# A mixture of experts in which every token goes through its two chosen experts only, by scattered and gathered rows, in place of all eight experts with gates

## The chip, the cores and the metric

The program runs on one core of one Trainium2 chip. The core has TensorE (PE: matmuls and transposes), VectorE (DVE), ScalarE (ACT), GpSimd (POOL), and SyncE (SP), whose queue issues most transfers; 16 DMA engines move the data. Each engine works through its own list of instructions in order and waits on semaphores. A time is the device time in microseconds (us) of one execution; a kernel's time is the median of its runs.

## The reference

x has 8 batches of 1,024 tokens of 128 numbers. Two blocks with residuals follow each other; shift, scale and gate of each come from a small conditioning row per batch (`mod`).

```
h = layernorm(x) * (1 + ca) + sa
x = x + ga * attention(h)                       # linear attention, 8 heads, RoPE, 5-tap convolution of v, output gate
h = layernorm(x) * (1 + cb) + sb
logits = h @ Wg + bg                            # 8 experts
probs = softmax(logits / 5.0)
vals, idx = top_k(probs, 2)
gates = mask / (sum(mask) + 1e-9)               # mask: vals at the two chosen experts, 0 elsewhere
y = sum over e of gates[e] * (gelu(h @ W1[e] + b1[e]) @ W2[e] + b2[e])
x = x + gb * y
```

W1 is 8 x 128 x 256 and W2 8 x 256 x 128. Six of a token's eight gates are zero. All inputs and the output are float32.

## The kernel before

All weights lie in SBUF, W1, W2 and the projections as a high and a low part (`w_h`, `w_l`) in the format float32r. `split` (L471 to L473) makes one product of full accuracy from three matmuls: high by high, low by high, high by low. A batch is 8 tiles (`J`) of 128 tokens, in two halves (`CH`) of 512 tokens (`CT`).

*Attention* runs in stages: statistics and normalisation of x (VectorE L834, L840, L846; the reciprocal root by `pow` on POOL, L755 and L758), transposes (L466), modulation on ScalarE into a high part and a copy (L639, L641), the low part on POOL (L771), the q, k, v projection per tile, the products with cosine and sine on VectorE (L878, L879) and their sum on POOL (L776), the k-v product (L502), denominators (L514) and numerators (L519), `heads` normalised by L910, five convolution steps (L1005, L1009), the gate, the output projection (L543) and x1 (L923). A second normalisation, transposes and logits (L558) follow, then the routing: softmax through tanh, a comparison of all pairs of experts, and the gates (L947 to L993).

*The experts* are 16 units a batch (`UNITS`): one half of the tokens by one expert. A unit is: layer 1 on PE (6 matmuls of 512 columns into `ps_h`), gelu on ScalarE (L702), multiplication by the gates on VectorE (L1019, `hid_g`; the gates come broadcast over all partitions from DRAM into `spread`), a high copy on ScalarE (L709, `hid_h`), the low part by subtraction on POOL (L807, `hid_l`), and layer 2 on PE (6 matmuls, L592 to L594), which adds up over the eight experts in `ps_y`. The result is turned back (L466) and added to x1 (L1030).

*The order* is written out by hand. A tick is one unit. `TICK` names the attention stages of the next batch that a tick issues, `LATE` the routing stages of the current one; layer 1 of a unit comes 8 ticks after its own tick (`SHIFT`), layer 2 three later (`LAG`). `schedule` (L141) walks all engines through the same ticks; the middle batches run in a hardware loop. Three PSUM banks (`ring`) go round among the attention stages.

## Time and profile before

| | us |
|---|---|
| three runs | 705.43, 706.93, 3041.11 |
| median | 706.93 |
| span of the profiled execution | 704.5 |

The span goes from the first to the last instruction; the page gives no time beside it for this execution, and the two close runs stand 0.9 and 2.4 us above it. The third run lies far off and no row explains it. A row of a group names line, engine, operation, what is written and read, the shape and the count; in a timeline the first number is the start in us and the second how long the row's instructions took together. VectorE is DVE in the rows, the queue of SyncE is SPq. A float32 matmul that isn't float32r leaves two records.

### The profile page before, as it was taken

How to read it: one execution, taken by the hardware profiler on the slowest of the kernel's cores; microseconds unless marked ns; L12 is line 12 of the kernel's file. 1: busy time of each engine (PE TensorE's matmuls, PEld its weight loads, DVE VectorE, ACT ScalarE, POOL GpSimd, SP SyncE). 2: the span in 40 equal slices, each digit the busy share in tenths (PEclk: the TensorE clock that was granted, in tenths of full speed). 3: DMA queues.
4: the chain of work that ended last, by engine and by line, in shares of the span. 5: the costliest groups of instructions: out<-in, count | busy, mean ns of one | idle time of the engine just before them, and what ended most of it. 6: DMA issues, size and time to landing. Idle time of an engine off the chain costs nothing.

```text
span 704.5 us, 9302 instructions
## 1 busy us (share of the span) xinstructions
PE 590.6 (84%) x2750; PEld 473.8 (67%) x2750; DVE 534.0 (76%) x1029; ACT 402.9 (57%) x639; POOL 450.5 (64%) x311
## 2 busy tenths in 40 slices
PE   4823897799987988789987989879887989889996
PEld 3623775587776866678765867668665777667884
DVE  5686677977889678787789778796798877884442
ACT  2331565566565746656565746657556655765773
POOL 3372555685866936857667838569458666665885
PEclk9975798899999989989999989999999989998999
DMA  6000341035100441008010341004210180004300
GB/s 239 2 30 0 127 125 31 1 98 168 45 1 15 128 124 45 1 17 247 15 30 14 113 138 45 1 15 158 91 45 0 34 230 15 1 15 169 96 16 15
DMA packets 37682, 47.57 MB, mean 68 GB/s; under 512 B 2096, under 2 KB 20432, under 8 KB 37392
## 3 DMA queue, kind: packets, MB, share of 16 engines
q1 hardware_dynamic: 37216, 46.77, 21.8%
q10 hardware_dynamic: 432, 0.43, 0.2%
q14 instruction: 23, 0.19, 0.1%
q8 instruction: 11, 0.18, 0.1%
HBM read 42.21 MB, written 4.98 MB: 67 GB/s over the span
## 4 chain that ended last, share of the span: by engine, by line
PE 30%; POOL 24%; DVE 21%; issue 17%; ACT 5%; POOLq 1%; DMA 1%; DVEq 0%; SPq 0%; ACTq 0%
POOL hid_l L807 20%; PE ring L466 4%; PE ring L519 3%; DVE xn L846 3%; DVE conv L1005 3%; DVE stats L834 3%; PE ps_y L592 3%; PE ring L514 3%; PE ps_y L593 3%; PE ps_y L594 2%; PE ps_h L471 2%; PE ps_h L472 2%; PE ps_h L473 2%; PE ring L558 2%; DVE hid_g L1019 2%
## 5 line engine op out<-in xcount | busy, mean ns | idle before, releaser
L807 POOL TENSOR_TENSOR hid_l<-hid_g,hid_h 128x1024 fp32r<-128x1024 f32 x128 | 304.9, 2389 | 147.4 <-ACT hid_h L709 138.4
L702 ACT ACTIVATE ps_h<-ps_h,b_f 128x512 f32<-128x512 f32 x256 | 158.5, 658 | 109.0 <-PE ps_h L473 108.3
L1019 DVE TENSOR_TENSOR hid_g<-ps_h,spread 128x1024 f32<-128x1024 f32 x128 | 155.5, 1216 | 71.1 <-POOL hid_l L807 58.2
L709 ACT ACTIVATE hid_h<-hid_g 128x1024 fp32r<-128x1024 f32 x128 | 135.5, 1058 | 11.7 <-DVE hid_g L1019 11.7
L592 PE MATMUL ps_y<-hid_h,w_h 128*128 128x512 f32 x256 | 114.3, 446 | 2.4 <-POOL hid_l L807 2.4
L471 PE MATMUL ps_h<-h_h,w_h 128*128 128x512 f32 x256 | 105.4, 412 | 9.2 <-DVE hid_g L1019 9.2
L593 PE MATMUL ps_y<-hid_h,w_l 128*128 128x512 f32 x256 | 106.0, 414 | 0.0
L594 PE MATMUL ps_y<-hid_l,w_h 128*128 128x512 f32 x256 | 105.8, 413 | 0.0
L472 PE MATMUL ps_h<-h_h,w_l 128*128 128x512 f32 x256 | 102.4, 400 | 0.0
L473 PE MATMUL ps_h<-h_l,w_h 128*128 128x512 f32 x256 | 102.1, 399 | 0.0
L466 PE MATMUL ring<-consts_f,xn 128*128 128x128 f32 x128 | 27.7, 362 | 63.4 <-DVE xn L846 62.2
L466 PEld LDWEIGHTS ring<-consts_f,xn 128*128 128x128 f32 x128 | 19.1, 182 | 73.2 <-DVE xn L846 58.1
L471 PEld LDWEIGHTS ps_h<-h_h,w_h 128*128 128x128 f32 x256 | 49.7, 194 | 24.5 <-DVE hid_g L1019 13.6
L592 PEld LDWEIGHTS ps_y<-hid_h,w_h 128*128 128x128 f32 x256 | 52.9, 207 | 16.0 <-POOL hid_l L807 3.7
L593 PEld LDWEIGHTS ps_y<-hid_h,w_l 128*128 128x128 f32 x256 | 52.0, 203 | 12.8 <-issue 3.0
L594 PEld LDWEIGHTS ps_y<-hid_l,w_h 128*128 128x128 f32 x256 | 51.4, 201 | 12.5
L472 PEld LDWEIGHTS ps_h<-h_h,w_l 128*128 128x128 f32 x256 | 49.4, 193 | 11.1 <-issue 0.2
L473 PEld LDWEIGHTS ps_h<-h_l,w_h 128*128 128x128 f32 x256 | 48.8, 191 | 11.8
L846 DVE TENSOR_SCALAR xn<-x,mean_var,rstd 128x128 f32<-128x128 f32 x64 | 54.7, 924 | 0.1
L776 POOL TENSOR_TENSOR qk<-qk_cos,qk_sin 128x256 f32<-128x256 f32 x64 | 46.7, 746 | 8.5 <-DVE qk_sin L879 8.4
L771 POOL TENSOR_TENSOR h_l<-heads,h_h 128x512 fp32r<-128x512 f32 x16 | 20.6, 1289 | 43.4 <-ACT heads L641 43.2
L1009 DVE SCALAR_TENSOR_TENSOR conv<-v_t,lepe_f,conv 128x1024 f32<-128x1024 f32 x32 | 44.2, 1382 | 0.3
(127 smaller groups left out, 929.9 us busy)
## 6 DMA issues: line engine op xcount, KB each, us to landing
spread<-gates_dram SPq DMA_DIRECT2D x16, 2048.0 KB, 8.9
xs<-in_x SPq DMA_DIRECT2D x8, 512.0 KB, 3.9
out<-y SPq DMA_DIRECT2D x16, 256.0 KB, 2.3
spread<-in_w SPq DMA_DIRECT2D x2, 1024.0 KB, 6.8
gates_e<-parts_dram SPq DMA_DIRECT2D x24, 32.0 KB
ga<-ga_dram SPq DMA_DIRECT2D x1, 512.0 KB, 3.6
spread<-in_wmod SPq DMA_DIRECT2D x1, 384.0 KB, 5.1
spread<-in_wqkvg ACTq DMA_DIRECT2D x1, 256.0 KB, 5.3
```

Of the source, the lines that this page charges most:

```text
L466: last = pe.transpose(dst[:, j * P:(j + 1) * P], src(j), ident)
L471: pe.matmul(dst, wh, ah, start=True, stop=False)
L472: pe.matmul(dst, wl, ah, start=False, stop=False)
L473: return pe.matmul(dst, wh, al, start=False, stop=True)
L592: pe.matmul(ps_y[:, :], w2_h[:, e, g, :], high, start=False, stop=False)
L593: pe.matmul(ps_y[:, :], w2_l[:, e, g, :], high, start=False, stop=False)
L594: last = pe.matmul(ps_y[:, :], w2_h[:, e, g, :], low, start=False, stop=(e == E - 1 and g == HH - 1))
L702: last = act.activation(bank, bank, ACT.Gelu, bias=b1_f[:, e, g:g + 1])
L709: act.activation(hid_h[n % 4][:, :, :], hid_g[n % 2][:, :, :], ACT.Copy)\
L807: pool.tensor_tensor(hid_l[n % 4][:, :, :], hid_g[n % 2][:, :, :], hid_h[n % 4][:, :, :].bitcast(F32), ALU.subtract).then_inc(s_hl, 1)
L846: last = dve.tensor_scalar(xn[:, j, :], src[:, j, :], mean_var[:, j, 0:1], rstd[:, j:j + 1], ALU.subtract, ALU.mult)
L1019: dve.tensor_tensor(hid_g[n % 2][:, :, :], ps_h[n % HIDDEN][:, :, :], gates_all[c][:, e, :].unsqueeze(1).to_broadcast([P, HH, CT]), ALU.mu ...
```

## The change

Nothing of the reference is left out. Attention keeps its computation, with some operations put together and more buffers. The routing finds the two chosen experts as two one-hot masks (`hot`), in `choose`. A prefix sum by matmuls (`prefix`) and `put` give each pair of token and choice a row number in a list ordered by expert, in which every expert's rows start at a multiple of 128. The list has 23 tiles of 128 rows for any choice (`TILES`). For each of 8 token tiles and 2 choices POOL scatters 128 rows of the normalised x1 to `x_sort` in DRAM (`scat`, 16 transfers a batch). SP loads the rows back in groups of four tiles (`xg`), and for each tile reads the expert's number from SBUF into a register and loads its W1, W2 and b1 (128 x 514 numbers) into one of 8 buffers (`w`). PE transposes the rows (`xsT`), ScalarE modulates them; layer 1, gelu and layer 2 run on tiles in pairs (`l1`, `l2`), with plain float32 matmuls of 128 columns and no gates. ScalarE evicts (`oev`), SP stores to `o_sort` (`ost`), POOL gathers two rows for each token (`gat`, 16 transfers), and VectorE multiplies them with the two gates and adds (`comb`, `fin`). The bias b2 comes by one matmul for each half. `AT` gives every stage its tick; batches start 24 ticks apart (`T`), the program has no loop, and within a tick the older batch comes first.

```diff
-TICK = {0: [], 1: ["norm1_0", "norm1_1"], 2: ["norm1_apply0", "norm1_apply1", "modulate"],
-        3: ["xT0"], 4: ["xT1", "qkv0"], 5: ["qkv1"], 6: ["qkv2"], 7: ["qkv3"], 8: ["vT"],
-        9: ["kv", "qT", "den_num"], 10: ["rdenT"], 11: ["gate"], 12: ["out0", "out1"],
-        13: ["norm2_apply0", "norm2_apply1"], 14: ["x1T0", "x1T1"], 15: ["logit"]}
...
-LATE = {0: ["softmax0"], 2: ["softmax1"], 3: ["rank0"], 4: ["rank1", "choice"], 5: ["gatesT"]}
...
+TILES = (TOP * S + E * (P - 1)) // P
+ROWS = TILES * P
+GROUP = 4
+GROUPS = -(-TILES // GROUP)
+PAIRS = -(-TILES // 2)
...
+T = 24
+FFN = 41
+AT = {"load": -24, "stat1_0": -6, "stat1_1": -5, "pow1": -5, "app1_0": -3, "app1_1": -3, "xT_0": -2, "xT_1": -1,
+      "qkv_0": 0, "qkv_1": 1, "qkv_2": 2, "qkv_3": 3, "vT": 4, "kv": 5, "qT": 5, "den": 6, "dn_0": 7, "dn_1": 7,
+      "conv_0": 8, "conv_1": 9, "conv_2": 10, "conv_3": 11, "gate": 11, "conv_4": 12,
+      "out_0": 13, "out_1": 14, "stat2_0": 15, "stat2_1": 16, "pow2": 16, "app2_0": 17, "app2_1": 18,
+      "x1T_0": 18, "x1T_1": 19, "logit": 20, "choose": 21, "prefix": 22, "soft": 23, "place": 24, "gT": 25}
+AT |= {f"scat_{j}": 28 + j for j in range(J)}
+AT |= {f"w_{t}": FFN + t - 3 for t in range(TILES)}
+AT |= {f"xg_{g}": (FFN - 3 + g if g < 3 else FFN - 1 + GROUP * (g - 3)) for g in range(GROUPS)}
+AT |= {f"xsT_{g}": FFN - 2 + GROUP * g for g in range(GROUPS)}
+AT |= {f"l1_{h}": FFN + 2 * h for h in range(PAIRS)}
+AT |= {f"l2_{h}": FFN + 2 * h + 3 for h in range(PAIRS)}
+AT |= {f"oev_{g}": FFN + GROUP * g + 6 for g in range(GROUPS)}
+AT |= {f"ost_{g}": FFN + GROUP * g + 7 for g in range(GROUPS)}
+AT |= {f"gat_{j}": 70 + j for j in range(J)}
+AT |= {"b2_0": 76, "b2_1": 81, "fin_0": 81, "fin_1": 85, "store_0": 82, "store_1": 86}
+AT |= {f"comb_{j}": 77 + j for j in range(J)}
+FIRST, LAST = min(AT.values()), max(AT.values())
+TABLE = {n: [name for name, at in AT.items() if at == n] for n in range(FIRST, LAST + 1)}
...
+def schedule(stage):
+    for tick in range(FIRST, T * (B - 1) + LAST + 1):
+        for b in range(B):
+            for name in TABLE.get(tick - T * b, []):
+                kind, _, n = name.partition("_")
+                stage(b, kind, int(n) if n else 0)
...
+                elif kind == "w":
+                    k = nth(b, n)
+                    if n == 0:
+                        sp.wait_ge(s_owner, b + 1)
+                    if k >= W_RING:
+                        old_b, old_t = divmod(k - W_RING, TILES)
+                        sp.wait_ge(s_l2, couple(old_b, old_t // 2) + 1)
+                    e = sp.value_load(owner[b % 2][0:1, n:n + 1], min_val=0, max_val=E - 1)
+                    sp.dma_start(wbuf[k % W_RING][:, :], w_all[bass.ds(e, 1)].rearrange("a p f -> (a p) f"))\
+                        .then_inc(s_wb[k % W_RING], 16)
+                elif kind == "xg":
+                    k, first = group(b, n), n * GROUP
+                    many = min(GROUP, TILES - first)
+                    if n == 0:
+                        sp.wait_ge(s_scat[b % 2], 16 * TOP * J * (b // 2 + 1))
+                    if k >= XG_RING:
+                        sp.wait_ge(s_xsT, k - XG_RING + 1)
+                    sp.dma_start(xg[k % XG_RING][:, 0:many, :],
+                                 x_sort[b % 2][first * P:(first + many) * P, :].rearrange("(t p) d -> p t d", p=P))\
+                        .then_inc(s_xg[k % XG_RING], 16)
+                elif kind == "ost":
+                    k, first = group(b, n), n * GROUP
+                    many = min(GROUP, TILES - first)
+                    sp.wait_ge(s_oe, k + 1)
+                    sp.dma_start(o_sort[b % 2][first * P:(first + many) * P, :].rearrange("(t p) d -> p t d", p=P),
+                                 o_s[k % O_RING][:, 0:many, :]).then_inc(s_os[k % O_RING], 16)
...
-            def layer1(f, n):
-                c, e = divmod(n, E)
-                if n == 0:
-                    pe.wait_ge(s_h2l, f.count(CH, CH))
-                if not (f.first and n < HIDDEN):
-                    pe.wait_ge(s_hg, f.count(UNITS, n + 1 - HIDDEN))
-                t = slice(c * CT, (c + 1) * CT)
-                for g in range(HH):
-                    w = slice(g * P, (g + 1) * P)
-                    last = split(ps_h[n % HIDDEN][:, g, :], w1_h[:, e, w], w1_l[:, e, w],
-                                 h2_h[f.par][:, t], h2_l[f.par][:, t])
-                last.then_inc(s_l1, 1)
...
-                pe.wait_ge(s_hl, f.count(UNITS, n + 1))
-                for g in range(HH):
-                    high, low = hid_h[n % 4][:, g, :], hid_l[n % 4][:, g, :]
-                    pe.matmul(ps_y[:, :], w2_h[:, e, g, :], high, start=False, stop=False)
-                    pe.matmul(ps_y[:, :], w2_l[:, e, g, :], high, start=False, stop=False)
-                    last = pe.matmul(ps_y[:, :], w2_h[:, e, g, :], low, start=False,
-                                     stop=(e == E - 1 and g == HH - 1))
-                last.then_inc(s_l2, 1)
...
+                elif kind == "xsT":
+                    k = group(b, n)
+                    pe.wait_ge(s_xg[k % XG_RING], ring_count(k, XG_RING))
+                    if k >= 1:
+                        pe.wait_ge(s_xs, k)
+                    for t in range(min(GROUP, TILES - n * GROUP)):
+                        last = pe.transpose(ps_x[:, t * P:(t + 1) * P], xg[k % XG_RING][:, t, :], ident)
+                    last.then_inc(s_xsT, 1)
+                elif kind == "l1":
+                    k, g = couple(b, n), group(b, 2 * n // GROUP)
+                    pe.wait_ge(s_xs, g + 1)
+                    if k >= 2:
+                        pe.wait_ge(s_gelu, k - 1)
+                    for m in couple_tiles(n):
+                        w = nth(b, m)
+                        pe.wait_ge(s_wb[w % W_RING], ring_count(w, W_RING))
+                        t = slice(m % GROUP * P, (m % GROUP + 1) * P)
+                        for h in range(HH):
+                            last = pe.matmul(ps_hid[k % 2][:, m % 2, h, :], wbuf[w % W_RING][:, h * P:(h + 1) * P],
+                                             xs_t[g % XS_RING][:, t], start=True, stop=True)
+                    last.then_inc(s_l1, 1)
+                elif kind == "l2":
+                    k, g = couple(b, n), group(b, 2 * n // GROUP)
+                    pe.wait_ge(s_gelu, k + 1)
+                    if g >= 1:
+                        pe.wait_ge(s_oe, g)
+                    for m in couple_tiles(n):
+                        w = nth(b, m)
+                        for h in range(HH):
+                            last = pe.matmul(ps_o[:, m % GROUP, :], hid[k % HID_RING][:, m % 2, h, :],
+                                             wbuf[w % W_RING][:, HID + h * D:HID + (h + 1) * D], start=(h == 0),
+                                             stop=(h == HH - 1))
+                    last.then_inc(s_l2, 1)
...
-            def high_part(f, n):
-                act.wait_ge(s_hg, f.count(UNITS, n + 1))
-                if not (f.first and n < 4):
-                    act.wait_ge(s_l2, f.count(UNITS, n - 3))
-                act.activation(hid_h[n % 4][:, :, :], hid_g[n % 2][:, :, :], ACT.Copy)\
-                    .then_inc(s_hh, 1)
...
+                elif kind == "l1":
+                    k = couple(b, n)
+                    act.wait_ge(s_l1, k + 1)
+                    if k >= HID_RING:
+                        act.wait_ge(s_l2, k - HID_RING + 1)
+                    for m in couple_tiles(n):
+                        w = wbuf[nth(b, m) % W_RING]
+                        for h in range(HH):
+                            last = act.activation(hid[k % HID_RING][:, m % 2, h, :], ps_hid[k % 2][:, m % 2, h, :],
+                                                  ACT.Gelu, bias=w[:, 2 * HID + h:2 * HID + h + 1])
+                    last.then_inc(s_gelu, 1)
...
-            def low_part(f, n):
-                pool.wait_ge(s_hh, f.count(UNITS, n + 1))
-                if not (f.first and n < 4):
-                    pool.wait_ge(s_l2, f.count(UNITS, n - 3))
-                pool.tensor_tensor(hid_l[n % 4][:, :, :], hid_g[n % 2][:, :, :],
-                                   hid_h[n % 4][:, :, :].bitcast(F32), ALU.subtract).then_inc(s_hl, 1)
...
+                elif kind == "scat":
+                    if n == 0:
+                        pool.wait_ge(s_slot, b + 1)
+                        if b == 0:
+                            pool.wait_ge(s_zero, 16 * 2 * GROUPS)
+                        if b >= 2:
+                            pool.wait_ge(s_xsT, group(b - 1, 0))
+                    for k in range(TOP):
+                        at = slots[b % 4][:, k * J + n:k * J + n + 1]
+                        pool.indirect_dma_start(x_sort[i], bass.IndirectOffsetOnAxis(ap=at, axis=0), xn2[i][:, n, :],
+                                                None).then_inc(s_scat[i], 16)
+                elif kind == "gat":
+                    if n == 0:
+                        for r in range(O_RING):
+                            pool.wait_ge(s_os[r], 16 * len(range(r, group(b + 1, 0), O_RING)))
+                        if b >= 1:
+                            pool.wait_ge(s_comb, J * b)
+                    for k in range(TOP):
+                        at = slots[b % 4][:, k * J + n:k * J + n + 1]
+                        pool.indirect_dma_start(og[:, k, n, :], None, o_sort[i],
+                                                bass.IndirectOffsetOnAxis(ap=at, axis=0)).then_inc(s_gat[n], 16)
...
-            def gate_hidden(f, n):
-                c, e = divmod(n, E)
-                if e == 0:
-                    dve.wait_ge(s_gall[c], f.count(16, 16))
-                dve.wait_ge(s_gelu, f.count(UNITS, n + 1))
-                if not (f.first and n < 2):
-                    dve.wait_ge(s_hl, f.count(UNITS, n - 1))
-                dve.tensor_tensor(hid_g[n % 2][:, :, :], ps_h[n % HIDDEN][:, :, :],
-                                  gates_all[c][:, e, :].unsqueeze(1).to_broadcast([P, HH, CT]),
-                                  ALU.mult).then_inc(s_hg, 1)
...
+            def choose(b):
+                dve.wait_ge(s_lg, b + 1)
+                step(b, 1, dve.tensor_tensor(logit[:, :, :], lg_ps.rearrange("p (j e) -> p j e", e=E), by_tile(br_f[:, :]),
+                                             ALU.add))
...
+                step(b, 13, dve.tensor_tensor(chosen[:, 0:J * E], hot[:, 0, :], hot[:, 1, :], ALU.add))
...
+            def put(b):
...
+                step(b, 34, dve.tensor_reduce(slots[b % 4][:, :], picked[:, :, :].rearrange("p k (j e) -> p (k j) e", e=E),
+                                              AX_X, ALU.add))
+                dve.sem_inc(s_slot, 1)
...
+                step(b, 37, dve.tensor_reduce(owner[b % 2][:, :], past[:, :, :], AX_X, ALU.add))
+                dve.sem_inc(s_owner, 1)
...
+                elif kind == "comb":
+                    c = n // JC
+                    dve.wait_ge(s_gat[n], 16 * TOP * (b + 1))
+                    if n % JC == 0:
+                        dve.wait_ge(s_b2, CH * b + c + 1)
+                    g = gate2[b % 4]
+                    dve.scalar_tensor_tensor(u[:, n, :], og[:, 0, n, :], g[:, 0, n:n + 1],
+                                             ps_z[:, n % JC * D:(n % JC + 1) * D], ALU.mult, ALU.add).then_inc(s_fin, 1)
+                    dve.wait_ge(s_fin, (J + CH) * b + c * (JC + 1) + n % JC + 1)
+                    dve.scalar_tensor_tensor(u[:, n, :], og[:, 1, n, :], g[:, 1, n:n + 1], u[:, n, :], ALU.mult, ALU.add)\
+                        .then_inc(s_comb, 1)
...```

The order on POOL, where the low part and the q-k sums of the next attention stand. Before, from one batch's experts:

```order
L807 TENSOR_TENSOR hid_l<-hid_g,hid_h 128x1024
L769 ISA
L771 TENSOR_TENSOR h_l<-heads,h_h 128x512
L804 REGISTER_ALU
L806 REGISTER_ALU
L807 TENSOR_TENSOR hid_l<-hid_g,hid_h 128x1024
L769 REGISTER_ALU
L771 TENSOR_TENSOR h_l<-heads,h_h 128x512
```

And in the changed kernel, one batch's steps from the powers to the last scatters (`og` is filled by gathers, `x_sort` by scatters; x2 is one token tile, x14 seven):

```order
L607 TENSOR_TENSOR rstd<-var_eps,minus_half 128x8
L652 DMA og<-o_sort,slots 128x128 x2
L622 TENSOR_TENSOR h_l<-h_f,h_h 128x512
L652 DMA og<-o_sort,slots 128x128 x2
L622 TENSOR_TENSOR h_l<-h_f,h_h 128x512
L652 DMA og<-o_sort,slots 128x128 x2
L626 TENSOR_TENSOR qk<-qk_cos,qk_sin 128x512
L652 DMA og<-o_sort,slots 128x128 x2
L626 TENSOR_TENSOR qk<-qk_cos,qk_sin 128x512
L652 DMA og<-o_sort,slots 128x128 x2
L626 TENSOR_TENSOR qk<-qk_cos,qk_sin 128x512
L652 DMA og<-o_sort,slots 128x128 x2
```

```order
L626 TENSOR_TENSOR qk<-qk_cos,qk_sin 128x512
L652 DMA og<-o_sort,slots 128x128 x2
L642 DMA x_sort<-xn_0,slots 2944x128 x2
L652 DMA og<-o_sort,slots 128x128 x2
L642 DMA x_sort<-xn_0,slots 2944x128 x14
L605 TENSOR_TENSOR var_eps<-mv,eps_ln 128x8
L607 TENSOR_TENSOR rstd<-var_eps,minus_half 128x8
```

The second piece follows the first without a gap. The subtractions of the experts are gone from POOL; between the low parts and the sums that attention needs stand gathers of a batch three further back, and ahead of the next power the scatters of the batch in between.

The order on PE beside the logits. Before:

```order
L471 MATMUL ps_h<-h_h,w_h 128x512
L472 MATMUL ps_h<-h_h,w_l 128x512
L473 MATMUL ps_h<-h_l,w_h 128x512
L558 MATMUL ring<-wr_f,heads 128x8 x8
L592 MATMUL ps_y<-hid_h,w_h 128x512
L593 MATMUL ps_y<-hid_h,w_l 128x512
L594 MATMUL ps_y<-hid_l,w_h 128x512
```

Changed:

```order
L409 MATMUL bank<-consts_f,xn_1 128x128 x4
L461 MATMUL ps_o<-wbuf,hid 128x128 x4
L417 MATMUL ps_z<-wr_f,h_t 128x8 x8
L450 MATMUL ps_hid<-xs_t,wbuf 128x128 x4
L461 MATMUL ps_o<-wbuf,hid 128x128 x4
```

Each unit of twelve matmuls of 512 columns has become a pair of tiles with four and four of 128.

## Rows read from the trace of the kernel before

**Rows 1.** The profile's page, part 1: busy us (share of the span), instructions.
```profile
PE 590.6 (84%) x2750; PEld 473.8 (67%) x2750; DVE 534.0 (76%) x1029; ACT 402.9 (57%) x639; POOL 450.5 (64%) x311
```

**Rows 2.** Stretches: length, busy us (PE, PEld, DVE, ACT, POOL), clock, DMA share, GB/s.
```profile
38.00:100.00 62.00, 36.23 (x176) 29.22 (x177) 47.35 (x114) 23.12 (x43) 29.49 (x27) 0.72 0.26 80
220.60:300.20 79.60, 69.57 (x332) 55.65 (x331) 62.77 (x117) 48.07 (x78) 54.65 (x38) 0.95 0.24 69
618.60:704.50 85.90, 74.40 (x303) 58.17 (x303) 40.34 (x40) 53.63 (x74) 58.20 (x26) 0.93 0.20 64
```

**Rows 3.** The timeline of SP's queue: start us, us, what is issued; loads of x.
```profile
106.16 0.41 SPq L395 DMA_DIRECT2D xs<-in_x  x1
...
515.15 0.38 SPq L395 DMA_DIRECT2D xs<-in_x  x1
```

**Rows 4.** Groups of instructions by line: busy us, mean ns of one; idle before.
```profile
L807 POOL TENSOR_TENSOR hid_l<-hid_g,hid_h 128x1024 fp32r<-128x1024 f32 x128 | 304.9, 2389 | 147.4 <-ACT hid_h L709 138.4 <-PE ps_y L594 8.5
...
L646 ACT ACTIVATE v<-ring 128x128 f32<-128x128 f32 x64 | 17.4, 279 | 37.5 <-DVE qk_sin L879 37.2
```

**Rows 5.** The timeline of PE (columns as in 3), five rows of one batch.
```profile
311.05 0.40 PE L471 MATMUL ps_h<-h_h,w_h 128*128 128x512 f32 x1
311.28 0.39 PE L472 MATMUL ps_h<-h_h,w_l 128*128 128x512 f32 x1
...
326.79 1.95 PE L502 MATMUL ring<-v,qk 128*128 128x129 f32 x16
328.57 1.04 PE L466 MATMUL ring<-consts_f,qk 128*128 128x128 f32 x8
329.36 0.48 PE L471 MATMUL ps_h<-h_h,w_h 128*128 128x512 f32 x1
```

**Rows 6.** Single lines on POOL: duration in ns min/median/max, first and last start.
```profile
L758 POOL TENSOR_TENSOR rstd<-var_eps,minus_half x32: 1006/1017/1104, 6.6 to 599.2; 128x4 f32<-128x4 f32 x32
...
L771 POOL TENSOR_TENSOR h_l<-heads,h_h x16: 1262/1294/1305, 13.9 to 554.1; 128x512 fp32r<-128x512 f32 x16
```

**Rows 7.** The timeline of DVE (VectorE), batch 0 and the next batch's start.
```profile
27.41 1.28 DVE L1009 SCALAR_TENSOR_TENSOR conv<-v_t,lepe_f,conv 128x1024 f32<-128x1024 f32 x1
...
63.75 0.22 DVE L965 TENSOR_TENSOR power<-root 128x64 f32<-128x64 f32 x1
64.01 0.87 DVE L834 BATCH_NORM_STATS2 stats<-xs 128x6 f32<-128x128 f32 x4
...
67.11 2.14 DVE L846 TENSOR_SCALAR xn<-xs,mean_var,rstd 128x128 f32<-128x128 f32 x8
```

**Rows 8.** The timeline of all engines, attention of batch 0.
```profile
23.53 1.48 POOL L776 TENSOR_TENSOR qk<-qk_cos,qk_sin 128x256 f32<-128x256 f32 x2 [0.19 <-DVE qk_sin L879]
...
35.23 1.29 DVE L910 TENSOR_TENSOR heads<-heads,ring 128x512 f32<-128x512 f32 x2 [0.79 <-PE ring L466]
```

**Rows 9.** The timeline of DVE: second normalisation and logits, batch 0 and a middle batch.
```profile
60.63 0.22 DVE L947 TENSOR_TENSOR logit<-ring,br_f 128x64 f32<-128x64 f32 x1 [2.96 <-PE ring L558]
...
353.77 6.07 DVE L846 TENSOR_SCALAR xn<-x,mean_var,rstd 128x128 f32<-128x128 f32 x7
...
366.11 0.22 DVE L947 TENSOR_TENSOR logit<-ring,br_f 128x64 f32<-128x64 f32 x1 [1.43 <-PE ring L558]
```

**Rows 10.** The timeline of DVE: batch 0's second normalisations, four and four.
```profile
43.72 1.11 DVE L846 TENSOR_SCALAR xn<-x,mean_var,rstd 128x128 f32<-128x128 f32 x4
...
44.90 9.39 DVE L846 TENSOR_SCALAR xn<-x,mean_var,rstd 128x128 f32<-128x128 f32 x4
```

**Rows 11.** DMA: two small issues on SP's queue, a busy stretch, landing of the output.
```profile
13.28 0.27 SPq L454 DMA_DIRECT2D ga_dram<-ga_row  x1
14.51 0.35 SPq L456 DMA_DIRECT2D ga<-ga_dram  x1
...
90.00:94.00 4.00, 4.00 (x20) 2.73 (x20) 3.97 (x6) 2.40 (x5) 0.00 (x0) 1.00 0.93 267
...
DMA to landing us min/median/max: 2.3/2.3/2.6
```

1352 lines of the change are left out of this document (565 added, 787 removed).

## The prediction

> **What bounds the kernel now.** I read the page's busy shares first. PE is the busiest engine, with VectorE behind it and GpSimd (POOL) third [rows 1]. In a middle stretch of 79.6 us PE works 69.6 us at a granted clock of 0.95, so it is close to full there; at both ends it is not [rows 2]. The queue of SyncE (SP) gives the period: the loads of x for batches 2 and 7 are issued at 106.2 and 515.2 us, so five batches take 409 us, 81.8 us each [rows 3]. In the last stretch, where only the experts are left, POOL is busy 58 us of 86, and its subtraction of 2.39 us for each of 128 units is what follows one after another [rows 2, 4]. The kernel is therefore bounded by PE with a POOL chain close behind, both by the work of eight experts on every token.
>
> The changed kernel removes that work and puts 256 row transfers on POOL's queue, so two questions decide: how long POOL needs for one, and what stands behind it in the queue.
>
> **PE, taken out and put in.** One split matmul of 512 columns follows the last at 0.23 us, and a batch has 192 of them in the experts: 44.5 us. A plain float32 matmul of 128 columns is two records; sixteen records take 1.78 us, so 0.22 us each [rows 5]. The 23 tiles have 92 of these, 20 us, and 23 transposes at 0.1 us; the two bias matmuls come to about 2 us. With attention and routing, some 18 us, PE has 43 to 45 us a batch at the full clock. With PE busy 58% of a stretch the clock was granted at 0.72 [rows 2], so I reckon with 50 us or more. PE stops being the bound.
>
> **VectorE.** It loses the 16 gate multiplications and gains routing. Routing is now 38 dependent steps; a step of 64 columns comes every 0.26 us (63.75 to 64.01) and the eight normalisations take 2.14 us [rows 7]. That makes 3.4 us for choosing the two experts (13 steps), 4.2 us for the softmax part (14, two with slow reciprocals), 3.3 us for the places (11). Combining is 16 operations in dependent pairs, 0.55 us a pair, and four operations of 0.69 us. Convolution is five of 1.28 us [rows 7]. With the rest I get about 47 us a batch.
>
> **ScalarE** has 46 activations of 128 columns at 0.28 us [rows 4], six to twelve evictions and the old work: 34 us, off the path.
>
> **DMA.** Weights are 23 times 263 KB, 6.05 MB a batch; the sorted rows written, read and written back, the gathers, x and the output bring it to 12.1 MB. At 0.93 of the engines' share 267 GB/s moved [rows 11], so a full share is about 285 and the batch takes 42 us: covered while a period is over 60 us. Eight weight buffers hide each landing. If the period fell to 50 us, this cover would be nearly gone.
>
> **SP.** Each tile needs a register loaded from SBUF, then a DMA. No row shows such a load. A small write, the wait for it and the next issue took 1.2 us from 13.28 to 14.51, and issuing alone 0.27 [rows 11]. I take 1.0 us and 0.4 for the issue, between 0.3 and 2.4: 32 us of queue a batch, and 3.2 us for a pair of tiles with its share of the other transfers.
>
> **POOL.** It loses 16 times 2.39 us, 38 us, and gets 32 indirect transfers of 128 rows. Call the price of one c. No row shows it. It can't well be below the 0.3 to 0.4 us of an issue by SP [rows 11], and from above I bound it by the 2.39 us of an operation on 1,024 columns [rows 4]. Nearest are the work of 4 columns that costs 1.02 us, mostly a fixed cost, and 512 columns at 1.29 [rows 6]. I take 1.3 us: 42 us a batch, 52 with what stays. That alone would hold a period of 55 us.
>
> But the queue is strict, and the order shown ahead puts two gathers before each of the steps that attention waits for. I follow one period from the logits' arrival. VectorE chooses (3.4), normalises the next batch (2.1), does the softmax (4.2) and the places (3.3): 13.0 us. The first low part can start on POOL at 7, after PE's transposes and ScalarE's two copies, and ends at 8.3. Then come, each behind the other, five pairs of gathers (13.0), the second low part (1.3) and four additions of cosine and sine products (5.2): 27.8 us. VectorE has only 6.6 us of work with these, so the rest is waiting. From the last addition to the end of the two normalised head products batch 0 took 11.5 us (25.0 to 36.5) [rows 8]; with expert matmuls between, I take 14. Convolution, the remaining combinations and sums fill 12 us. Output projection, x1, statistics, POOL's power and the second normalisation take 9.5. From there to the next logits the steady state shows 6.3 us (359.8 to 366.1) [rows 9]. The period is 27.8 + 14 + 12 + 9.5 + 6.3 = 69.6 us. Meanwhile POOL has 20 more transfers, 26 us, before its next power, against 35 us; that leaves it in time up to c of about 1.75.
>
> **Ends.** Batch 0's logits came at 60.6 us [rows 9]; four normalisations beside POOL's splitting of the weights took 9.4 us where four others took 1.1 [rows 10], and this splitting is gone: 52 us. The first period has no gathers and no experts, 58 us; the second no gathers, 63; five full ones, 348. After the last logits POOL has gathers of batch 5 and scatters of batch 7, 32c = 42 us; landing, loading and turning 6; twelve pairs of tiles at 3.3 us, 40, set by SP and PE together; eviction and store 3.5, the store landing in 2.3 us [rows 11]; 16 gathers, 21; combining and the last store 6. That is 119.
> Sum: 52 + 58 + 63 + 348 + 119 = 640 us of span. The profiled execution spans 704.5 us and the median of the runs is 706.9, 2.4 more, so I say **642 us**, 9% below.
>
> At c = 1.0 the same sum gives 614; at 0.4, where VectorE sets the additions, about 570; at 1.5 about 660; at 1.8 about 710.
>
> **A rule against the change.** Beside a POOL operation VectorE's normalisation grew from 0.33 to several us each: four took 9.4 us [rows 10]. So the two engines lock each other out. In that trace VectorE paid and POOL's own operations kept their length (L771 1.26 to 1.31 us) [rows 6].
> The Trainium skill, page "SBUF — State Buffer", section "Who interferes with whom", says that GpSimd and a VectorE operation in a two-port mode exclude each other, and its box on DMAs from GpSimd adds that descriptors can't be written meanwhile. The trace agrees on the exclusion; it has no DMA from GpSimd for the rest.
>
> **Rivals.**
> 1. *Stalls overlap.* If the queues slide so far apart that the waits fall under each other, the fullest queue rules: POOL 52 us, PE and VectorE 47 to 50, so a period of 55. Then 52 + 50 + 55 + 5 × 55 + 107 = 539, 541 us with the 2.4. For it: each engine has its own program, and only data holds them together. Against it: before, PE at 70 us a batch already made a period of 82 [rows 2, 3]. Chance 0.17.
> 2. *POOL becomes the bound: slower.* At c = 2.0 the additions end at 34.8 and 20 more transfers last to 74.8, later than VectorE needs the power; 9.7 follow. Period 84.5, five are 422, the last part 153 and the sum 52 + 60 + 66 + 422 + 153 = 753, 755 us. It decides from c = 1.8. For it: 128 addresses must be worked out one by one, and 1.02 us for 4 columns shows a slow engine. Against: no row on POOL near this size is over 1.3. Chance 0.22.
> 3. *SP's register loads.* At 2.2 us each a tile takes 2.6 and a batch's queue 66 us, about a period; the twelve last pairs take 27 us more. 670 to 690 us. Chance 0.07.
> 4. *The lock-out hits the row transfers.* If both times eight normalisations (4.3 us a batch) stop POOL where attention waits, seven batches lose 30 us: 672 us. Chance 0.05.
> The cited section would have it so.
>
> That the change does not cut the work can be left out: the number of matmuls is fixed in the program.
>
> **Numbers.** My case has 0.49, from 610 to 690 us; the rivals 0.17, 0.22, 0.07 and 0.05. No change, as measured here, means within 2%, 693 to 721 us. Faster takes nearly all of my case, the first rival and the two small ones less a part that goes with c above 1.6: 0.70. The edge between mine and the second gives 0.09 for the same, and 0.21 stays for slower. The range reaches from 560, where c is 0.4 and some stalls overlap, to 755.
>
> **What would show it.** Right: POOL's indirect transfers at 1.1 to 1.6 us; the additions waiting behind gathers; PE's busy share near 0.7 with a lower clock; loads of x 68 to 72 us apart in the middle; about 110 to 120 us from batch 7's logits to the end. Wrong: transfers of 2 us or more, or POOL without idle time; VectorE over 90% busy, with short waits (first rival); SP always late with weights (third); normalisations stretched beside transfers (fourth).

## The result, and the profile after

In the first comparison the changed kernel took **795.9 us** (792.5 to 800.4, four executions) and the kernel before 706.2: ratio 1.128 [1.120, 1.135]. I had said 642, from 560 to 755. The profiled execution spans 794.0 us.

The same program was then run on other chips. On some it takes 671 to 674 us, 5% less than the kernel before; on others about 799 again. The document is about this difference, and then about the 30 us that separate 671 from 642.

The page of the changed kernel, first comparison (columns as in [rows 1] and [rows 4]):

```profile
PE 488.0 (61%) x2888; PEld 421.8 (53%) x2888; DVE 367.5 (46%) x1151; ACT 254.8 (32%) x678; POOL 343.7 (43%) x342
...
DVE 24%; another core or an unknown queue 20%; issue 17%; PE 16%; POOL 10%; ACT 7%; DMA 4%; SPq 2%; POOLq 0%; DVEq 0%; ACTq 0%
...
L652 POOL DMA_INDIRECT og<-o_sort,slots x128 | 122.9, 960 | 117.1 <-DMA o_sort<-o_s 71.4
...
L642 POOL DMA_INDIRECT x_sort<-xn,slots x128 | 125.9, 984 | 38.7 <-issue 38.7
```

The loads of x on SP's queue, to be held against [rows 3], first comparison and then c_rep1 (a run of the same program, below):

```profile
297.85 0.51 SPq L265 DMA_DIRECT2D xs<-in_x  x1
...
386.39 0.51 SPq L265 DMA_DIRECT2D xs<-in_x  x1
```

```profile
275.08 0.51 SPq L265 DMA_DIRECT2D xs<-in_x  x1
...
346.82 0.51 SPq L265 DMA_DIRECT2D xs<-in_x  x1
```

The two rows of a pair are 88.5 and 71.7 us apart. Over three intervals in the middle (from 208.53 to 473.88 us, and from 200.03 to 423.28) it is 88.5 and 74.4 us a batch, where it was 81.8 before and I had 68 to 72. In the first comparison no engine is busy for more than 61% of the span, and no engine is the bound. A gather takes 0.96 us and a scatter 0.98, each with 0.30 of issue ahead of it: 1.27 us from one to the next, where I had c = 1.3. POOL idles, too. What is new is the second entry of the chain: 20% of the span was waited for a releaser that the profile can't name.

The timeline of the middle batch whose logits stand at 463.51 us, same execution. It begins with the last addition of cosine and sine products on POOL (L626) and ends where VectorE has multiplied both head products (L804):

```profile
402.15 1.27 POOL L626 TENSOR_TENSOR qk<-qk_cos,qk_sin 128x512 f32<-128x512 f32 x1
...
408.82 1.92 PE L375 MATMUL bank<-ksum_s,q_t 128*128 128x8 f32 x16
...
411.07 1.06 PE L450 MATMUL ps_hid<-xs_t,wbuf 128*128 128x128 f32 x8
...
411.96 1.02 PE L381 MATMUL bank<-q_t,kv_s 128*128 128x512 f32 x2
...
416.34 0.22 DVE L797 TENSOR_SCALAR den<-bank 128x64 f32<-128x64 f32 x1 [8.07 <-remote]
...
418.77 1.92 PE L381 MATMUL bank<-q_t,kv_s 128*128 128x512 f32 x2
...
427.60 1.14 ACT L574 ACTIVATE hid<-ps_hid,wbuf 128x128 f32<-128x128 f32 x4 [6.95 <-issue]
427.88 0.97 POOL L642 DMA_INDIRECT x_sort<-xn,slots  x1 [0.30 <-issue]
...
431.84 1.27 ACT L544 ACTIVATE heads<-bank,v_sum 128x512 f32<-128x512 f32 x2 [2.61 <-remote]
432.56 0.69 DVE L804 TENSOR_TENSOR heads<-heads,bank 128x512 f32<-128x512 f32 x1 [14.86 <-ACT heads L544]
...
433.87 0.69 DVE L804 TENSOR_TENSOR heads<-heads,bank 128x512 f32<-128x512 f32 x1 [0.62 <-PE bank L386]
```

Three pairs are to be read, each a group of matmuls and its reader; whatever else the reader waits for in the code was done long before:

- the denominators: matmuls (L375) end at 410.7, VectorE reads (L797) at 416.3, 5.6 us later;
- an expert's hidden units: matmuls (L450) end at 412.1, ScalarE reads (L574) at 427.6; it was free from 420.7, so 7 us of this is pure waiting;
- the first numerators: matmuls (L381) end at 413.0, ScalarE reads (L544) at 431.8, 19 us later. In ScalarE's order the hidden units and an eviction stand ahead of this read; its own wait is the last 2.6 us.

The last reader starts 3 us after the last scatter of POOL's block has ended (428.85). The same stretch on a chip where the program takes 671 to 674 us (run c_rep1, below), with the same lines:

```profile
438.76 1.27 POOL L626 TENSOR_TENSOR qk<-qk_cos,qk_sin 128x512 f32<-128x512 f32 x1
...
445.39 1.92 PE L375 MATMUL bank<-ksum_s,q_t 128*128 128x8 f32 x16
...
447.35 0.22 DVE L797 TENSOR_SCALAR den<-bank 128x64 f32<-128x64 f32 x1 [2.50 <-PE bank L375]
...
447.64 1.06 PE L450 MATMUL ps_hid<-xs_t,wbuf 128*128 128x128 f32 x8
...
448.53 1.02 PE L381 MATMUL bank<-q_t,kv_s 128*128 128x512 f32 x2
...
449.91 1.13 ACT L574 ACTIVATE hid<-ps_hid,wbuf 128x128 f32<-128x128 f32 x4
...
451.39 1.30 ACT L544 ACTIVATE heads<-bank,v_sum 128x512 f32<-128x512 f32 x2
...
451.72 0.97 POOL L642 DMA_INDIRECT x_sort<-xn,slots  x1 [0.30 <-issue]
...
452.99 0.69 DVE L804 TENSOR_TENSOR heads<-heads,bank 128x512 f32<-128x512 f32 x1 [0.16 <-PE bank L386]
```

Here every reader follows at once, or as soon as its engine is free (ScalarE works from 449.25 to 452.7 without a pause), with POOL's transfers running beside it just as densely. From the last addition to the last L804 it is 13.7 us here and 31.1 there.

Two more views of the first comparison. The list of waits, those that end with an unknown releaser (us in total, times, longest):

```profile
ACT hid L574 <- remote: 61.9, 6, 18.7
...
DVE den L797 <- remote: 61.4, 6, 17.9
...
DVE u L837 <- remote: 39.3, 1, 39.3
...
ACT xs_t L564 <- remote: 21.7, 5, 10.1
...
DVE heads L804 <- remote: 15.6, 1, 15.6
...
ACT heads L544 <- remote: 11.2, 6, 3.6
```

Each of these instructions reads a result of TensorE and waits for its semaphore (L837 and L804 wait for something else besides). In c_rep1 this list is empty. The totals aren't all stall: a wait that c_rep1 has under the name of PE is counted with its whole length. So it is with the 39.3 us of L837 in the tail, for which c_rep1 has 35.9 us. And the stretches around the stall (columns as in [rows 2]):

```profile
404.00:412.00 8.00, 8.00 (x61) 7.95 (x60) 1.04 (x4) 1.08 (x2) 6.17 (x7) 0.82 0.17 50
412.00:420.00 8.00, 3.12 (x10) 1.41 (x8) 1.29 (x4) 1.28 (x3) 6.10 (x7) 0.82 0.28 83
420.00:428.00 8.00, 0.69 (x1) 0.00 (x0) 0.00 (x0) 1.05 (x3) 5.94 (x7) 0.50 0.15 49
```

TensorE, VectorE and ScalarE stand still from 420.7 to 427.6 while POOL goes on; the 16 DMA engines are 15% busy. The granted clock is at its lower level, 1.2 GHz, from 420 on. It had fallen before: the second numerators (L381 at 418.77), behind TensorE's pause from 413.0 to 417.9, take 1.92 us where the first (411.96) took 1.02. So the matmuls did not run on unseen, as far as the clock tells: their records end at 413 and what comes late is the signal. The ends of matmuls in the trace are modelled, so this is a strong reading and no proof.

### The profile page after: what moved, and what is told of

Same layout as the page of the kernel before. It is cut to its first block, busy times and chain, and to the rows that moved or that the text cites. A ratio compares the mean times of both kernels' runs of the same rounds, so it can differ in the third digit from the quotient of the medians.

```text
span 794.0 us, 9999 instructions
## 1 busy us (share of the span) xinstructions
PE 488.0 (61%) x2888; PEld 421.8 (53%) x2888; DVE 367.5 (46%) x1151; ACT 254.8 (32%) x678; POOL 343.7 (43%) x342
## 4 chain that ended last, share of the span: by engine, by line
DVE 24%; another core or an unknown queue 20%; issue 17%; PE 16%; POOL 10%; ACT 7%; DMA 4%; SPq 2%; POOLq 0%; DVEq 0%; ACTq 0%
POOL og L652 5%; DVE heads L763 5%; PE ps_o L461 3%; ACT hid L574 3%; PE ps_hid L450 3%; POOL qk L626 3%; DVE xn L673 2%; DVE stats L662 2%; PE bank L361 2%; DMA wbuf<-in_w_all 2%; DMA xg<-x_sort 1%; POOL rstd L607 1%; ACT o_s L582 1%; PE bank L402 1%
## 5 line engine op out<-in xcount | busy, mean ns | idle before, releaser
L652 POOL DMA_INDIRECT og<-o_sort,slots x128 | 122.9, 960 | 117.1 <-DMA o_sort<-o_s 71.4
L574 ACT ACTIVATE hid<-ps_hid,wbuf 128x128 f32<-128x128 f32 x368 | 105.6, 370 | 208.7 <-PE ps_hid L450 126.0
L461 PE MATMUL ps_o<-wbuf,hid 128*128 128x128 f32 x736 | 120.7, 316 | 53.8 <-ACT o_s L582 34.2
L461 PEld LDWEIGHTS ps_o<-wbuf,hid 128*128 128x128 f32 x736 | 110.3, 228 | 66.4 <-ACT hid L574 66.1
L642 POOL DMA_INDIRECT x_sort<-xn,slots x128 | 125.9, 984 | 38.7 <-issue 38.7
L450 PE MATMUL ps_hid<-xs_t,wbuf 128*128 128x128 f32 x736 | 119.0, 308 | 18.0 <-DMA wbuf<-in_w_all 11.0
L450 PEld LDWEIGHTS ps_hid<-xs_t,wbuf 128*128 128x128 f32 x736 | 106.9, 220 | 29.3 <-issue 14.3
L605 POOL TENSOR_TENSOR var_eps<-mv,eps_ln 128x8 f32<-128x8 f32 x16 | 3.2, 203 | 207.3 <-DVE mv L667 207.3
L837 DVE SCALAR_TENSOR_TENSOR u<-og,gate,ps_z 128x128 f32<-128x128 f32 x64 | 21.4, 335 | 116.9 <-PE ps_z L468 53.4
L386 PE MATMUL bank<-consts_f,qk 128*128 128x128 f32 x64 | 16.2, 404 | 90.1 <-ACT heads L544 53.6
L386 PEld LDWEIGHTS bank<-consts_f,qk 128*128 128x128 f32 x64 | 11.0, 205 | 108.1 <-issue 96.4
L564 ACT ACTIVATE xs_t<-ps_x,mod 128x512 f32<-128x512 f32 (+1 forms) x48 | 36.5, 761 | 55.8 <-PE ps_x L438 31.4
L763 DVE SCALAR_TENSOR_TENSOR heads<-v_t,lepe_f,heads 128x1024 f32<-128x1024 f32 x40 | 51.2, 1281 | 0.5
L804 DVE TENSOR_TENSOR heads<-heads,bank 128x512 f32<-128x512 f32 x16 | 11.0, 687 | 85.4 <-ACT heads L544 51.5
L626 POOL TENSOR_TENSOR qk<-qk_cos,qk_sin 128x512 f32<-128x512 f32 x32 | 41.0, 1281 | 19.4 <-DVE qk_sin L786 18.9
L622 POOL TENSOR_TENSOR h_l<-h_f,h_h 128x512 fp32r<-128x512 f32 x16 | 20.4, 1274 | 59.8 <-ACT h_f L514 58.3
L520 ACT ACTIVATE v<-bank 128x128 f32<-128x128 f32 x64 | 17.4, 283 | 52.7 <-DVE qk_sin L786 40.0
```

The source lines that it names most:

```text
L386: last = pe.transpose(of(f"rden_{n}", b)[:, j * P:(j + 1) * P], rden_x[:, k:k + HEADS, :].rearrange("p h d -> p (h d)"), ident)
L450: last = pe.matmul(ps_hid[k % 2][:, m % 2, h, :], wbuf[w % W_RING][:, h * P:(h + 1) * P], xs_t[g % XS_RING][:, t], start=True, stop=True)
L461: last = pe.matmul(ps_o[:, m % GROUP, :], hid[k % HID_RING][:, m % 2, h, :], wbuf[w % W_RING][:, HID + h * D:HID + (h + 1) * D], start=(h ...
L564: act.activation(xs_t[k % XS_RING][:, 0:many * P], ps_x[:, 0:many * P], ACT.Identity, bias=mod[:, 3, b:b + 1], scale=mod[:, 4, b:b + 1]).t ...
L574: last = act.activation(hid[k % HID_RING][:, m % 2, h, :], ps_hid[k % 2][:, m % 2, h, :], ACT.Gelu, bias=w[:, 2 * HID + h:2 * HID + h + 1])
L626: pool.tensor_tensor(qk[:, 2 * n:2 * n + 2, :], qk_cos[n % 2][:, :, :], qk_sin[n % 2][:, :, :], ALU.add)\
```

## The experiments

**One part left out at a time.** Each was thought of as the test of a cause (the theories A, B, C are in the first text); all ran on one chip.

```diff
 e_noscat                                   (POOL raises s_scat itself)
-  pool.indirect_dma_start(x_sort[i], IndirectOffsetOnAxis(at), xn2[i][:, n, :], None)
 e_nogat                                    (og zeroed once, POOL raises s_gat)
-  pool.indirect_dma_start(og[:, k, n, :], None, o_sort[i], IndirectOffsetOnAxis(at))
 e_wstatic
-  e = sp.value_load(owner[b % 2][0:1, n:n + 1], ...); sp.dma_start(wbuf, w_all[bass.ds(e, 1)])
+  sp.dma_start(wbuf, w_all[n % E])
 e_nowload
+  if k >= W_RING: return                   (only the first 8 tiles of weights)
```

e_noscat: 

> Leaves out the 128 scatters; x_sort keeps its zeros, and POOL raises the scatters' semaphore itself after the last place in its order. Theory A (POOL's block of 18 to 20 transfers a batch holds back what waits for TensorE, some 17 us of each 88 us period): the time from the last q-k addition to the normalised heads falls from 31 to about 14 us, the period to about 70, the whole to 660 to 700 us. Theory B (the weight DMAs and register loads on SP make the stall, the scatters only stand beside it): 775 to 796 us. Theory C (late instruction fetch in a longer program): 780 to 796 us, since the instructions left are nearly as many.

e_nogat: 

> Leaves out the 128 gathers (og is zeroed once, POOL raises the gathers' semaphores itself). Theory A: the 16 scatters are still a block of 20 us, but the four gathers inside it are gone and those ahead of h_l too, so the stall shrinks by about 5 us and the first part of the period by up to 5: period 78 to 82, the whole 715 to 760 us. Theories B and C: 785 to 796 us, less only the tail's last gathers (10 us).

e_wstatic: 

> The weight DMA takes expert n mod 8 by a fixed address, no register load on SP; bytes and number of DMAs are the same (each tile gets the wrong expert's weights). Theory A: within 8 us of the change, 785 to 800 us. Theory B in the form that the register loads or the dynamic address are the cause: about 690 us. Theory C: 785 to 800 us.

e_nowload (its "batch 2" counts from one): 

> Only the first 8 weight tiles are ever loaded; all later tiles use what lies in the ring, and 176 of 184 weight DMAs of 257 KB are left out, with their register loads. Theory A in its plain form (POOL's transfers alone are enough): 775 to 800 us, the stall between additions and heads stays at 17 us. Theory B (the weight traffic is needed for the stall, which would fit that batch 2 had scatters without weight traffic and no stall): stall gone, 670 to 700 us. Theory C: 775 to 796 us.

Measured, one execution each: 668.4, 631.4, 668.1 and 655.0 us. In none of the four does a wait end with an unknown releaser. Four unlike edits seemed to cure the whole stall, which no theory of mine allowed. That sent me to a control.

**The change as it is, and edits that change nothing of the load.** 
```diff
 c_late
+  dve.memset(og[:, :, :, :], 0.0)          (once, at the start)
 c_place                                    (ahead of x_sort and o_sort)
+  spare = dram("spare", (ROWS + 37, D))
 c_half                                     (og zeroed once)
-  for k in range(TOP):                     (around the gather)
+  for k in range(1):
```

c_same: 

> The change again, as it is: a control. If the stall belongs to the program it takes 788 to 802 us here too, and TensorE's increments come late again. If it belongs to the chip or the moment of the first run, about 690 us (what the four kernels with one part left out would lead to, with the part put back: 668 + about 20).

c_late: 

> The change with one more instruction of VectorE at the start (og is zeroed, as in the run without gathers). Theory D (the stall needs scatters, gathers and register-addressed weights together, by their load): 788 to 802 us. Theory E (the stall hangs on an accident of timing or placement, and any small edit may take it away, which would explain why each of four different parts left out removed all of it): near 690 us with no late increments.

c_place: 

> The change with one more DRAM tensor of 1.5 MB ahead of x_sort and o_sort, so that these lie elsewhere, and one small DMA in the start. Theory D: 788 to 804 us. Theory E in its form of placement: near 690 us.

c_half: 

> Gathers only of the first choice: 64 instead of 128, og zeroed once. Theory D with a dose: between the change (796) and the run without gathers (631), with a stall still in most batches, 700 to 760 us. Theory E, or a threshold in the number of transfers: no stall, 645 to 665 us.

Measured: 671.4, 675.3, 674.4 and 627.8 us (kernel before 707.9 beside them); c_half came out below both of its ranges. The control itself has no stall. So the four runs above say nothing on its cause, and c_late and c_place neither; they hold for a chip without it.

**Repeated, five rounds each, two chips.**

c_rep1: 

> The change again, in five rounds beside the kernel before. Theory F (the first comparison met a disturbance from outside the program, and 671 us is the change's own time): 665 to 680 us, ratio 0.94 to 0.96, no late increments. Theory G (the program has two ways to run, and which one is met changes from one execution to the next): some of the executions near 795 us and some near 671. Theory D: 788 to 802 in all.

c_rep2: 

> The change once more in five rounds, to see whether its 796 us comes back anywhere. Theory F (a disturbance outside the program): 665 to 680 us, ratio 0.94 to 0.96. Theory G (the chip decides): on a chip of the first kind 788 to 802 us in all rounds with late increments of TensorE, on another 665 to 680.

c_rep1, on the chip of c_same: 673.5 us (669.2 to 678.0, six executions), ratio **0.953 [0.949, 0.957]**. c_rep2, on another: 798.8 us (793.3 to 800.6, five), ratio **1.131 [1.129, 1.134]**. The kernel before beside them: 706.8 and 706.4. D and E fall: the program without an edit runs both ways. Theory G in the form "the chip decides" fits all executions, none of one kind having been met on a chip of the other. F falls as far as it means a single disturbance, for the loss came back in all five rounds. But each chip with the stall was met in one session only (the chip of c_rep1 in two, without it both times), so something that lay beside the program in that session, and left the kernel before alone, isn't ruled out. "Chip" stands below for both.

**With a control on the same chip.**

d_control: 

> The change again, as the control of this chip. On a chip like those of the first comparison and of c_rep2 788 to 802 us with TensorE's increments up to 20 us late; on a chip like that of c_same and c_rep1 665 to 680 us with none late.

d_wstatic: 

> Weights by a fixed address, no register load, all 184 weight DMAs kept (each tile gets the wrong expert's weights). If the control shows the stall: theory P (POOL's transfers with any weight traffic beside them) 780 to 800 us; theory Q (POOL's transfers beside register loads and register-addressed DMAs of SP) 665 to 680 us, nothing late. If the control shows none: 660 to 675 us.

d_nowload: 

> Only the first 8 weight tiles are loaded, all later tiles use what lies in the ring. If the control shows the stall: theories P and Q both give 650 to 665 us; a stall that remains (770 to 800) would say that POOL's transfers alone make it once TensorE has the experts' matmuls to do. If the control shows none: 650 to 660 us.

d_noscat: 

> Leaves out the 128 scatters, x_sort keeps its zeros. If the control shows the stall: the 17 us between additions and heads are gone, but the gathers, also a run of transfers beside the same traffic, may hold some increments, 680 to 720 us. If the control shows none: 660 to 675 us.

Measured: 674.3, 670.5, 652.9 and 662.9 us. This chip, too, has no stall, so P and Q were not told apart; but the price of scatters, weights and register loads without the stall is now measured beside a control, in one execution each; six executions of the change in c_rep1 spread over 9 us.

f_wstatic, beside f_spread2 as a control: 

> The change with weights by a fixed address and no register loads (each tile gets the wrong expert's weights). On a chip with the stall (f_spread2 near 845): theory Q (register-addressed DMAs are needed for it) 665 to 680 us, theory P (any weight traffic) 780 to 800 us. On a chip without it: 665 to 673 us for the third time.

Measured: **790.0 us** (786.3 and 793.7), ratio 1.120 [1.113, 1.127], on a chip where the control shows the stall (848 us). Theory Q falls: register-addressed weights are not needed for it. The timeline of f_wstatic, middle batch, same instructions as above (their lines are one lower):

```profile
404.54 1.27 POOL L625 TENSOR_TENSOR qk<-qk_cos,qk_sin 128x512 f32<-128x512 f32 x1
...
409.57 1.92 PE L374 MATMUL bank<-ksum_s,q_t 128*128 128x8 f32 x16
...
412.71 1.02 PE L380 MATMUL bank<-q_t,kv_s 128*128 128x512 f32 x2
...
415.96 0.23 DVE L796 TENSOR_SCALAR den<-bank 128x64 f32<-128x64 f32 x1 [6.94 <-remote]
...
428.69 0.69 ACT L543 ACTIVATE heads<-bank,v_sum 128x512 f32<-128x512 f32 x1 [2.61 <-remote]
...
434.35 1.38 DVE L803 TENSOR_TENSOR heads<-heads,bank 128x512 f32<-128x512 f32 x2 [17.02 <-remote]
```

**Gathers put elsewhere.** v_spread keeps all transfers and moves the gathers off the way of attention; v_spread2 also moves four combines. Both add the waits that ps_z and o_sort then need, and move the ticks of `b2`, `fin` and `store` along.

```diff
-AT |= {f"gat_{j}": 70 + j for j in range(J)}
+AT |= {f"gat_{j}": 80 + j if j < 4 else 89 + (j - 4) // 2 for j in range(J)}
-AT |= {f"comb_{j}": 77 + j for j in range(J)}
+AT |= {f"comb_{j}": 85 + j if j < 4 else 95 + j for j in range(J)}     # v_spread
+AT |= {f"comb_{j}": 91 if j < 4 else 95 + j for j in range(J)}         # v_spread2
```

v_spread: 

> All 32 transfers a batch are kept, but the gathers stand elsewhere in POOL's order: eight of them behind the scatters, eight between norm2's and the next norm1's pow, none between h_l and the q-k additions; combines, b2 and final steps move with them. In the change four gathers stand between h_l and the last addition, at 1.27 us each, and the run without gathers had a period 5.2 us shorter there (68.2 against 73.4 us). Theory: 6 to 7 periods lose 5 us each, 635 to 650 us, ratio 0.90 to 0.92. Rival: the block behind the additions grows to 24 transfers (30.5 us) and holds norm2's pow (needed some 31 us after the additions), or the later combines delay the tail: 665 to 690 us.

v_spread2: 

> As v_spread, but the first four combines stand behind norm2's application instead of ahead of x1's second half. In v_spread the first part of the period was 5 us shorter as expected, and the stretch from the gate product to norm2's end rose from 10.3 to 15.9 us, since VectorE waited there in its order for gathers at the end of the 24-transfer block. Theory: that stretch is back at 10 to 12 us, the period 68 to 70, the whole 640 to 655 us. Rival: norm2's pow itself waits for the block of 24 transfers on POOL, 665 to 680 us.

f_spread2: 

> v_spread2 again, as it is: gathers behind the scatters and behind norm2's pow, combines behind norm2. On a chip with the stall 835 to 855 us, as on the first. On a chip without it the first theory is tested for the first time: stretch from gate product to norm2's end 10 to 12 us, period 68 to 70, 635 to 655 us, ratio 0.90 to 0.93; rival (pow waits for the 24-transfer block) 665 to 680 us.

v_spread, beside c_rep1: 676.2 us, ratio 0.957 [0.954, 0.960], no gain over the change: the theory's 635 to 650 did not come, its rival's 665 to 690 did. Its gathers no longer stand ahead of the additions, but VectorE now waits for them between gate product and x1:

```profile
458.62 0.35 DVE L843 SCALAR_TENSOR_TENSOR u<-og,gate,ps_z 128x128 f32<-128x128 f32 x1 [3.35 <-DMA og<-o_sort,slots]
...
462.68 0.35 DVE L843 SCALAR_TENSOR_TENSOR u<-og,gate,ps_z 128x128 f32<-128x128 f32 x1 [1.41 <-DMA og<-o_sort,slots]
```

v_spread2 met chips with the stall both times: 845.0 us, 1.200 [1.194, 1.205], and 848.0 us, 1.200 [1.194, 1.205]. What it is worth without the stall isn't known. With it, it costs 46 us more than the change on the same chip (798.8). Its block behind the additions has 24 transfers, the change's 20, which is 5 us more of them; from the last addition to the normalised heads a middle batch takes 38.2 us (421.6 to 459.8) against 31.1. So the stall was longer with the longer block; that is one pair of programs, which differ in the combines too.

## Why the prediction was wrong

**The step that failed** is "from the last addition to the end of the two normalised head products ... I take 14". It was 31 us in the first comparison. Read from the logits on, the middle periods were (us; means of four, from the timelines):

| stretch | predicted | first comparison | c_rep1 |
|---|---|---|---|
| logits to last addition | 27.8 | 28.2 | 28.2 |
| to normalised heads | 14 | 30.9 | 14.2 |
| to the end of the gate product | 12 | 13.2 | 13.2 |
| to the end of norm2 | 9.5 | 8.8 | 11.0 |
| to the next logits | 6.3 | 6.9 | 7.2 |
| period | 69.6 | 87.9 | 73.8 |

Against my sum of 640 the first comparison's span of 794.0 has 12 us more up to batch 0's logits (63.7), 14 in the next two batches, 91 in the five full periods (439 against 348) and 37 behind the last logits (155.7 against 119). Between the two executions lie 119 us: 10 up to batch 2's logits (189.0 against 199.2), 69 in the next five periods (to 559.1 and 638.3), 40 behind the last logits (115.7 against 155.7), where experts' matmuls stand beside POOL's transfers as well. My 14 is right on a chip without the stall. I had asked only what POOL's transfers hold up on POOL's queue, and in my fourth rival what VectorE does to them; that they could hold up what waits for TensorE was in no case. The trace of before could not show it, for it has no transfer on POOL.

The Trainium skill, page "SBUF — State Buffer", section "Who interferes with whom", says of the access to SBUF that TensorE and ScalarE never wait for another engine. The chips without the stall agree (empty list of unknown releasers in c_rep1). On the others TensorE's readers are late by up to 19 us beside POOL's transfers, and for the time the measurement decides; whether access to SBUF is what holds them no run shows.

**What the stall needs** is known in part. It comes with a chip: in the first comparison (which chip that was isn't on record) and on the two chips of c_rep2 and f_spread2, never on the three others. The chip of the first four experiments is counted among these, since e_wstatic shows no stall there (668.1 us) and f_wstatic does where the stall is. Late signals were met only of matmuls that ran beside POOL's transfers, and the last signal came when a block was over: in the first comparison 2.7 to 4.7 us behind it (readers at 169.10, 431.84, 682.68 and 739.68, last transfers ended at 166.4, 428.9, 678.0 and 736.8). But no program without the transfers was run on such a chip, so that they are needed is argued, not shown. Nor is it the signal alone. Behind the last logits TensorE itself halts between matmuls of one tile, where the code has no wait; c_rep2 and f_wstatic show the same there, c_rep1 and d_control don't:

```profile
670.07 0.88 PE L450 MATMUL ps_hid<-xs_t,wbuf 128*128 128x128 f32 x5
672.78 0.27 PE L450 MATMUL ps_hid<-xs_t,wbuf 128*128 128x128 f32 x1 [1.83 <-issue]
674.88 0.37 PE L450 MATMUL ps_hid<-xs_t,wbuf 128*128 128x128 f32 x1 [1.83 <-issue]
```

Scatters alone are not enough: batch 0's (86.2 to 107.8 us in the first comparison) run beside batch 1's attention, and there the reader L797 starts at 91.73, right behind its matmuls. Batch 1's (from 146.4) do it, and by then the first experts' matmuls and weights are under way; no gather has run yet. Register addresses are not needed (f_wstatic). Whether it is the weight traffic or the experts' matmuls wasn't tried on such a chip, and stays open. Nor is it settled what in the chip differs. Late fetching of instructions is out: in the first comparison no packet of it falls in 408 to 432 us.

**The price of a transfer** held: 1.27 us against 1.3. So the second rival (POOL the bound from 1.8) did not happen, although its 755 us was nearest to the first result.

**The other rivals.** Stalls do not overlap: the middle period stays at 73.8 us without the stall, not 55. SP sets nothing (next point). The lock-out of the fourth rival isn't there for normalisations: eight keep their 2.14 us in c_rep1. It is there for other operations of VectorE. Beside the convolution scatters grow from 0.97 to 1.54 us and once to 2.0 (25 of 128 are over 1.1 us), and the combining operation L840 takes 2.00 us beside an addition on POOL (434.52) where its median is 0.35. I had named the wrong operation; the scatters lie behind the additions, where nothing waits for them.

**SP's register load** I took at 1.0 us, with 0.4 for the issue. In c_rep1 four loads in a row (116.05 us, 3.70 together) come 1.12 us apart, 0.33 of it the issue, so a register costs about 0.8: near my size, and off the path. Without register loads the change took 670.5 against 674.3 us, and 668.1 on another chip. These 4 us are less than the spread of the change itself.

**Without the stall** c_rep1's span of 674.8 us compares with my 640. Fill: batch 0's logits at 65.5, I had 52 (+13.5). The additions end at 30.6 us against 25.0 before, and the convolution, which before ran ahead of the heads (27.41 in [rows 7]), now follows them with 6.6 us; I subtracted VectorE's lock-out [rows 10] and forgot both. The lock-out itself went, as said: eight normalisations take 2.14 us. The next two batches: 123.5 against 121. Then five periods of 74.0, not 69.6 (+22), the excess in the last three stretches. In that to the end of norm2 experts' matmuls stand between the two halves of the output projection, which run at the lower clock (393.03 and 396.60 us, 2.07 and 1.91 us for eight records); I had no term for that, and how the excess divides wasn't tested. Tail: 115.7 against 119.

**Scatters and weights.** Left out, the scatters are worth 11 us (662.9 against 674.3), little for 128 of them and hardly more than the spread: they lie in the shadow that I gave them. The weight DMAs with their register loads are worth 21 us (652.9 against 674.3), where I had their traffic fully covered.

**Gathers** are worth some 40 us (631.4 without them, on a chip without a control; 627.8 with half of them, against 671.4), the largest part. The timeline of POOL in c_rep1 shows why; two of them stand ahead of each step that attention waits for:

```profile
429.16 0.96 POOL L652 DMA_INDIRECT og<-o_sort,slots  x1 [0.16 <-issue]
430.43 0.94 POOL L652 DMA_INDIRECT og<-o_sort,slots  x1 [0.30 <-issue]
431.39 1.30 POOL L626 TENSOR_TENSOR qk<-qk_cos,qk_sin 128x512 f32<-128x512 f32 x1
432.85 0.96 POOL L652 DMA_INDIRECT og<-o_sort,slots  x1 [0.16 <-issue]
434.11 0.95 POOL L652 DMA_INDIRECT og<-o_sort,slots  x1 [0.30 <-issue]
435.08 1.28 POOL L626 TENSOR_TENSOR qk<-qk_cos,qk_sin 128x512 f32<-128x512 f32 x1
```

With one gather in each of these places, as in c_half, four periods take 274.0 us (logits at 251.4 and 525.4), 68.5 each, and with none 68.3 (256.1 and 529.2 in e_nogat): so one gather in each place costs nothing and the second of each pair is what costs. Held against c_rep1, c_half has 29 us less in the five full periods and 15 less behind the last logits, where half of the last gathers are gone (100.6 against 115.7).

## What to carry to other kernels

Ask of a block of transfers on POOL not only what stands behind it in POOL's queue, but who else waits for anything while it runs; a mechanism that the trace of before can't show still deserves a chance. When several unlike edits "cure" a loss, run the unedited kernel beside them before believing any. A kernel with long runs of row transfers beside matmuls is to be timed on more than one chip.

## What the runs showed of the hardware

- Chips, or what lay beside the program on them, differ. One program takes 671 to 674 us on two chips and 796 to 799 us in the first comparison and on another; a kernel without transfers on POOL takes 704 to 708 us on all of them.
- On the slower kind a reader of TensorE starts up to 19 us after the matmuls' records end, while POOL's indirect transfers keep their 1.27 us each.
- An indirect transfer of 128 rows of 512 bytes costs POOL 0.96 us and 0.30 of issue on either kind of chip. Beside VectorE's convolution a scatter took 1.54 us, at most 2.0 (c_rep1).
